# Cross-attention kernel: turned probabilities passed through DRAM, loads in five pieces, stores moved in SP's order

## The chip, the cores and the metric

The kernel runs on one core of a Trainium2 chip. A time is the device time in microseconds of one execution. The kernel before takes 877.26 us, the median of three runs (876.62 to 878.73).

## What is computed

8 batches of 1024 tokens with 640 features attend to 56 text tokens and 8 image tokens, with 20 heads of 32 features and two softmaxes, whose results are added:

```python
q = _split_heads(hidden_states @ w_q, HEADS)
k, v = _split_heads(text @ w_k, HEADS), _split_heads(text @ w_v, HEADS)
out_text = _merge_heads(_sdpa(q, k, v))
k_ip, v_ip = _split_heads(ip_h @ w_k_ip, HEADS), _split_heads(ip_h @ w_v_ip, HEADS)
out_ip = _merge_heads(_sdpa(q, k_ip, v_ip, mask=mask_ip))
out = (out_text + IP_SCALE * out_ip) @ w_out + b_out + residual
```

## The kernel before, in words

**Groups.** The work is cut into NG = 16 groups of GQ = 512 tokens, two for each batch (GPB = 2). Features lie on the partitions. The 640 features are KD = 5 blocks of 128, and each block holds four heads. A matmul of full precision is made of three (L99 to L102): every operand is split into a high part, rounded by ACT, and a low part, the difference, taken by DVE or POOL.

**Chunks.** The scores of one block of features are a chunk of `prob`: 128 tokens on the partitions, 1024 columns (4 token tiles, 4 heads, 64 keys). A chunk m of group g goes through ACT (`copy_scores`, L203), POOL (mask and `sub_max`, L243, L249), DVE (`maxima`, L216), ACT (`exponentials`, L208), DVE (`sums`, L222) and POOL (`normalise`, L256). The product with V needs keys on the partitions, so the chunk must be turned. `turn` (DVE, L229 to L237) transposes it in squares of 32 into a slot of `stage`, and `hand_over` (SP, L454 to L463) moves the squares to their partitions by DMA, back into the chunk's place in `prob`. It does this in three shares, `SHARES`: chunks 0 and 1, chunks 2 and 3, chunk 4. Each share takes 16 DMAs (4 source quadrants by 4 target quadrants), and one semaphore for each share, `pT_landed`, is met when all 16 have landed.

**After landing.** For each of ten pairs of heads (p = 2m, 2m + 1), `pT_part` on ACT (L717 to L720) waits for the share, rounds the pair into `pT_hi` (ring of 4), and POOL (L573, odd p) or DVE (L946, even p) writes `pT_lo`. `pv_pair` on PE (L1166, L1167) multiplies both with `v_parts`. `move_pv` (ACT, L725) and `add_pv` (DVE, L956) put the pair together, `oT_part` on ACT (L729) and POOL (L569) splits it, and `out_step` on PE multiplies with the output weights. `output` on DVE (L958 to L962) adds bias and residual into `res`, and SP stores it.

**One pass of PE's loop** (L1205 to L1227), for group g: pairs 0 and 1 of group g, the scores of chunk 0 of g + 1, the rest of the output product of g - 1 (39 wide matmuls), then four times two pairs, the scores of the next chunk, 9 output matmuls of g and 15 query matmuls of g + 2, and 15 more query matmuls at the end. So the softmax of g + 1 runs beside the products of g, and the pass of g + 1 begins with the pairs of its chunk 0.

**Every engine's order is written by hand.** DVE in a pass: the low parts of x for g + 2, outputs of g - 1, `turn(g, 4)` (L1001), then `turn(n, 0)` and `turn(n, 1)` of n = g + 1 (L1012, L1013), `turn(n, 2)` (L1028), and at the end `pT_part(n, 0)`, `pT_part(n, 2)`, `turn(n, 3)` (L1030 to L1032). SP, which issues nearly all DMAs, in a pass:

```python
hand_over(g, 2)                      # chunk 4 of g
for m in OUT_ORDER: store(g - 1, m)  # five stores, each waits for its output
...                                  # first pass of a batch: load_k, load_v
hand_over(g + 1, 0)                  # chunks 0 and 1
load_x(g + 3); load_res(g)           # one DMA of 1280 KB each
hand_over(g + 1, 1)                  # chunks 2 and 3
```

`load_x(g)` waits for the low parts of the x that had the buffer before (L466); `load_res(g)` waits for all stores before it (L470). A wait on SP holds everything queued behind it.

Of the kernel before, what the change touches and what calls it, by code (L numbers as in the profile page):

```python
# [5 lines left out]
F32 = mybir.dt.float32  # L6
F32R = mybir.dt.float32r
ACT = mybir.ActivationFunctionType
ALU = mybir.AluOpType
# [17 lines left out]
S_RING = 4  # L27


def attention_kernel(nc, xT_dram, textT, ipT, bbox, w_q, w_k, w_v, w_k_ip, w_v_ip, w_out, b_out, grid_x, grid_y, outT):  # L30
# [24 lines left out]
    k_scratch = nc.dram_tensor("k_scratch", (P, B, KD * KEYS), F32).ap()  # L55
    v_scratch = nc.dram_tensor("v_scratch", (TT, D), F32).ap()
# [3 lines left out]
    with whole:  # L60
# [108 lines left out]
        res_loaded, stored = sem("res_loaded"), sem("stored")  # L169

        SHARES = ((0, 2), (2, 4), (4, 5))
        pT_landed = [sem(f"pT_landed{i}") for i in range(len(SHARES))]

        def landed(eng, g, m):

            share = min(m // 2, len(SHARES) - 1)
            wait(eng, pT_landed[share], 16 * QUADS * QUADS * (g + 1))
# [48 lines left out]
        def stage_slot(m):  # L226
            return min(m, S_RING - 1)

        def turn(dve, g, m):  # L229

            before = (g, 3) if m == 4 else (g - 1, 4) if m == 3 else (g - 1, m)
            dve.wait_ge(prob_done, KD * g + m + 1)
            if before[0] >= 0:
                landed(dve, *before)
            src = prob[:, m * CHUNK:(m + 1) * CHUNK].rearrange("p (t c i) -> p t c i", t=GT, i=QUAD)
            dst = stage[:, stage_slot(m)].rearrange("p c (t i) -> p t c i", i=QUAD)
            nc.vector.transpose(dst, src).then_inc(turned, 1)  # L237
# [43 lines left out]
        stage = sb("stage", [P, S_RING, 2 * QUADS, P])  # L281
# [104 lines left out]
        def pT(p):  # L386

            return prob[:, p * GQ:(p + 1) * GQ]

        def pT_at(t, g, p):  # L390
            return t[:, (PAIRS * g + p) % P_RING, :]

# [23 lines left out]
        with nc.Block() as block:  # L416

            @block.sync
            def _(sp):
# [34 lines left out]
                def hand_over(g, share):  # L454
                    m0, m1 = SHARES[share]
                    turns = stage[:].rearrange("p s (h c) t -> p (s h) c t", c=QUADS)
                    pairs = prob[:].rearrange("p (n q t) -> p n q t", q=QUADS, t=P)
                    s0 = 2 * stage_slot(m0)
                    sp.wait_ge(turned, KD * g + m1)
                    for q in range(QUADS):  # L460
                        for c in range(QUADS):
                            sp.dma_start(pairs[c * QUAD:(c + 1) * QUAD, 2 * m0:2 * m1, q, :],  # L462
# [803 lines left out]
```

## Time and profile before

| what | value |
| --- | --- |
| median of the runs | 877.26 us |
| profiled execution | 873.89 us |
| its span, first to last instruction | 872.1 us |
| PE busy (matmul) | 814.0 us, 93% |
| DVE, POOL, ACT busy | 670.6, 624.1, 541.3 us |
| mean granted TensorE clock | 0.976 |
| DMA moved | 128.08 MB, mean 147 GB/s |

The profile is of one execution. Busy time is time in which an engine works on an instruction; issuing a DMA doesn't count as busy, and stands under SPq in the chain and in the timeline. The idle time of an engine is put down to what released it. The chain is the path of work that ended last, followed back step by step. A granted clock of 1.00 is 2.4 GHz, half of it 1.2 GHz.

### The profile page before, as it was taken

To read this page: it belongs to the slowest core of one execution; us is meant where nothing else is said; L and a number is where in the kernel's file an instruction comes from. 1 tells how busy PE (TensorE), PEld (TensorE's weight loads), DVE (VectorE), ACT (ScalarE), POOL (GpSimd) and SP (SyncE) were. 2 spreads that over 40 slices of the span, in tenths; PEclk is the share of its full clock that TensorE was granted. 3 is DMA by queue.
4 is the path that set the end of the run, shared out by engine and by line. 5 is a ranking of instruction groups with operands and counts; after the bars stand their busy time and mean duration, and the time that the engine had idled before them with its cause. 6 is when DMAs were issued, how large, how long until landed. Compare 5 with 4: busy or idle time off the path is not lost.

```text
span 872.1 us, 13091 instructions
## 1 busy us (share of the span) xinstructions
PE 814.0 (93%) x4381; PEld 650.9 (75%) x4381; DVE 670.6 (77%) x983; ACT 541.3 (62%) x928; POOL 624.1 (72%) x576
## 2 busy tenths in 40 slices
PE   9999779999989998999989998999989998998586
PEld 8899558787868776787868776887867786885464
DVE  7758578888868796888868796888868796987853
ACT  7766267675766666665656666667757666675531
POOL 0069349696959786787959786887959697887841
PEclk9999989999999999899999999999999999999898
DMA  9933343536362725446462726445463626252525
GB/s 324 378 94 119 108 126 89 176 115 187 113 194 52 232 57 165 143 120 181 120 192 57 225 55 182 130 127 170 133 192 100 191 88 212 58 177 62 176 61 193
DMA packets 138867, 128.08 MB, mean 147 GB/s; under 512 B 17072, under 2 KB 101040, under 8 KB 138672
## 3 DMA queue, kind: packets, MB, share of 16 engines
q1 hardware_dynamic: 138656, 125.93, 48.4%
q10 hardware_dynamic: 144, 1.31, 0.4%
q8 instruction: 35, 0.57, 0.3%
q14 instruction: 32, 0.26, 0.1%
HBM read 61.32 MB, written 23.59 MB: 97 GB/s over the span
## 4 chain that ended last, share of the span: by engine, by line
SPq 45%; DVE 17%; PE 15%; DMA 11%; issue 7%; ACT 4%; POOL 1%; ACTq 0%; DVEq 0%
SPq L462 39%; DMA xin<-in_xT 6%; DVE res L962 4%; SPq L497 4%; DVE xT_lo L117 3%; PE bank L100 3%; DVE stage L237 3%; PE bank L101 3%; PE bank L102 3%; DMA res<-in_xT 2%; DVE o_raw L956 2%; DMA prob<-stage 2%; PE bank L196 1%; ACT xT_hi L113 1%; DVE top L216 1%
## 5 line engine op out<-in xcount | busy, mean ns | idle before, releaser
L573 POOL TENSOR_TENSOR pT_lo<-prob,pT_hi 128x512 fp32r<-128x512 f32 x80 | 116.4, 1455 | 99.9 <-ACT pT_hi L720 99.6
L725 ACT ACTIVATE pv_part<-bank 64x512 f32<-64x512 f32 x160 | 94.7, 592 | 148.2 <-PE bank L1167 145.8
L249 POOL TENSOR_TENSOR prob<-prob,top 128x896 f32<-128x896 f32 (+1 forms) x160 | 179.4, 1142 | 4.5 <-DVE top L216 4.1
L256 POOL TENSOR_TENSOR prob<-prob,inv 128x896 f32<-128x896 f32 (+1 forms) x160 | 172.6, 1101 | 11.3 <-DVE inv L224 10.6
L100 PE MATMUL bank<-oT_hi,wo_hi 128*128 128x512 f32 x400 | 168.9, 422 | 8.3 <-POOL oT_lo L569 4.7
L100 PE MATMUL bank<-xT_hi,wq_hi 128*128 128x512 f32 x400 | 156.0, 390 | 5.8 <-ACT qT L139 3.2
L101 PE MATMUL bank<-oT_lo,wo_hi 128*128 128x512 f32 x400 | 159.1, 398 | 0.0
L102 PE MATMUL bank<-oT_hi,wo_lo 128*128 128x512 f32 x400 | 158.6, 396 | 0.0
L101 PE MATMUL bank<-xT_lo,wq_hi 128*128 128x512 f32 x400 | 155.6, 389 | 0.0
L102 PE MATMUL bank<-xT_hi,wq_lo 128*128 128x512 f32 x400 | 155.6, 389 | 0.0
L569 POOL TENSOR_TENSOR oT_lo<-o_raw,oT_hi 128x512 fp32r<-128x512 f32 x80 | 109.9, 1374 | 61.9 <-ACT oT_hi L729 60.6
L956 DVE TENSOR_TENSOR o_raw<-bank,pv_part 64x512 f32<-64x512 f32 x160 | 110.1, 688 | 55.6 <-ACT pv_part L725 52.8
L720 ACT ACTIVATE pT_hi<-prob 128x512 fp32r<-128x512 f32 x160 | 93.4, 623 | 78.0 <-DMA prob<-stage 77.2
L946 DVE TENSOR_TENSOR pT_lo<-prob,pT_hi 128x512 fp32r<-128x512 f32 x80 | 73.5, 919 | 56.3 <-ACT pT_hi L720 55.3
L222 DVE TENSOR_REDUCE total<-prob 128x16 f32<-128x896 f32 (+1 forms) x160 | 101.7, 676 | 4.4 <-ACT prob L208 4.2
L100 PEld LDWEIGHTS bank<-oT_hi,wo_hi 128*128 128x128 f32 x400 | 76.8, 192 | 36.6 <-ACT prob L203 7.3
L1166 PE MATMUL bank<-pT_hi,v_parts 128*128 128x512 f32 x160 | 67.5, 422 | 38.9 <-DVE pT_lo L946 28.4
L196 PEld LDWEIGHTS bank<-k_diag,qT 64*128 64x128 f32 x1280 | 81.7, 196 | 28.7 <-issue 21.4
L216 DVE TENSOR_REDUCE top<-prob 128x16 f32<-128x896 f32 (+1 forms) x160 | 99.6, 664 | 2.1 <-POOL prob L243 1.3
L237 DVE STREAM_TRANSPOSE stage<-prob 128x1024 f32<-128x1024 f32 x80 | 97.2, 1224 | 1.4
L196 PE MATMUL bank<-k_diag,qT 64*128 64x128 f32 x1280 | 97.0, 294 | 0.1
L203 ACT ACTIVATE prob<-bank 128x512 f32<-128x512 f32 x160 | 85.5, 592 | 11.3 <-PE bank L196 11.1
(103 smaller groups left out, 1247.8 us busy)
## 6 DMA issues: line engine op xcount, KB each, us to landing
prob<-stage SPq DMA_DIRECT2D x512, 64.0 KB, 2.0
res<-in_xT SPq DMA_DIRECT2D x16, 1280.0 KB, 9.3
outT<-res SPq DMA_DIRECT2D x80, 256.0 KB, 2.6
xin<-in_xT SPq DMA_DIRECT2D x15, 1280.0 KB, 6.3
prob<-stage SPq DMA_DIRECT2D x256, 32.0 KB, 1.9
w_raw<-in_L_xattn_w_k SPq DMA_DIRECT2D x8, 320.0 KB, 4.9
w_raw<-in_L_xattn_w_k_ip SPq DMA_DIRECT2D x8, 320.0 KB, 5.3
w_raw<-in_L_xattn_w_v_ip SPq DMA_DIRECT2D x8, 320.0 KB, 4.3
```

Of the source, the lines that this page charges most:

```text
L100: nc.tensor.matmul(dst, a_hi, b_hi, start=first, stop=False)
L101: nc.tensor.matmul(dst, a_hi, b_lo, start=False, stop=False)
L102: return nc.tensor.matmul(dst, a_lo, b_hi, start=False, stop=last)
L196: ins = nc.tensor.matmul(s_bank(g, 2 * m + r)[:, t * PW:(t + 1) * PW], qT[rows, m, q_cols], k_diag[rows, m, :], start=True, stop=True)
L216: ins = nc.vector.tensor_reduce(top[:, m, n, :], chunk(m)[:, :, k0:k1], AX.X, ALU.max)
L237: nc.vector.transpose(dst, src).then_inc(turned, 1)
L249: ins = nc.gpsimd.tensor_tensor(s, s, top[:, m, n, :].unsqueeze(2).broadcast_to([P, ROWS, k1 - k0]), ALU.subtract)
L256: ins = nc.gpsimd.tensor_tensor(s, s, inv[:, m, n, :].unsqueeze(2).broadcast_to([P, ROWS, k1 - k0]), ALU.mult)
L462: sp.dma_start(pairs[c * QUAD:(c + 1) * QUAD, 2 * m0:2 * m1, q, :], turns[q * QUAD:(q + 1) * QUAD, s0:s0 + 2 * (m1 - m0), c, :]).then_inc( ...
L569: nc.gpsimd.tensor_tensor(oT_at(oT_lo, g, m), o_raw[:, (KD * g + m) % 2, :], oT_at(oT_hi, g, m).bitcast(F32), ALU.subtract).then_inc(oT_lo ...
L573: nc.gpsimd.tensor_tensor(pT_at(pT_lo, g, p), pT(p), pT_at(pT_hi, g, p).bitcast(F32), ALU.subtract).then_inc(pT_lo_pool, 1)
L956: nc.vector.tensor_tensor(by_quadrant(raw), a, c, ALU.add).then_inc(pv_added, 1)
```

## The change

Turned chunks take another way. `write_out` sends one whole stage slot (128 partitions of 4 KB, 512 KB) to a DRAM tensor `p_scratch` in one DMA; `read_back` waits until it has landed and brings it into the chunk's place in four DMAs of 128 KB, one for each quadrant of keys, in runs of 1 KB where `hand_over` before had runs of 512 bytes. To make such runs, `turn` writes its slot in the order quadrant, half, token, and a pair's columns in `prob` are then four runs of 128 instead of one of 512; `pT`, `pT_part_at` and the three `pT_part` follow that. `hand_over` writes all its chunks and then reads them back. There is a `pT_landed` for each chunk. `stage` has three slots in turn instead of four, and `turn` waits for the write of three chunks before (`in_dram`) instead of a landing. The loads of x (from group 2 on) and of the residual are five DMAs each of 256 KB, and stores and residual loads have a semaphore for each block. In SP's pass, `load_x(g + 3)` and the five stores now come ahead of chunk 4's `hand_over`, the residual loads right behind it, and then K and V and the two other `hand_over` calls.

```diff
--- before
+++ after
@@ -24,7 +24,7 @@
 P_RING = 4
-S_RING = 4
+S_RING = 3
@@ -53,6 +53,7 @@
     k_scratch = nc.dram_tensor("k_scratch", (P, B, KD * KEYS), F32).ap()
+    p_scratch = nc.dram_tensor("p_scratch", (KD, P, CHUNK), F32).ap()
     v_scratch = nc.dram_tensor("v_scratch", (TT, D), F32).ap()
@@ -166,15 +167,15 @@
             sem(n) for n in ("mask_added", "max_subbed", "prob_done", "pT_lo_pool", "oT_lo_done"))
-        res_loaded, stored = sem("res_loaded"), sem("stored")
-
-        SHARES = ((0, 2), (2, 4), (4, 5))
-        pT_landed = [sem(f"pT_landed{i}") for i in range(len(SHARES))]
+        res_loaded, stored = [sem(f"res_loaded{m}") for m in range(KD)], [sem(f"stored{m}") for m in range(KD)]
+        written = [sem(f"written{i}") for i in range(S_RING)]
+        pT_landed = [sem(f"pT_landed{m}") for m in range(KD)]
         def landed(eng, g, m):
-
-            share = min(m // 2, len(SHARES) - 1)
-            wait(eng, pT_landed[share], 16 * QUADS * QUADS * (g + 1))
+            wait(eng, pT_landed[m], 16 * QUADS * (g + 1))
+
+        def in_dram(eng, n):
+            wait(eng, written[n % S_RING], 16 * (n // S_RING + 1))
@@ -223,17 +224,13 @@
-        def stage_slot(m):
-            return min(m, S_RING - 1)
-
         def turn(dve, g, m):
-            before = (g, 3) if m == 4 else (g - 1, 4) if m == 3 else (g - 1, m)
-            dve.wait_ge(prob_done, KD * g + m + 1)
-            if before[0] >= 0:
-                landed(dve, *before)
-            src = prob[:, m * CHUNK:(m + 1) * CHUNK].rearrange("p (t c i) -> p t c i", t=GT, i=QUAD)
-            dst = stage[:, stage_slot(m)].rearrange("p c (t i) -> p t c i", i=QUAD)
+            n = KD * g + m
+            dve.wait_ge(prob_done, n + 1)
+            in_dram(dve, n - S_RING)
+            src = prob[:, m * CHUNK:(m + 1) * CHUNK].rearrange("p (t h c i) -> p t h c i", t=GT, h=2, i=QUAD)
+            dst = stage[:, n % S_RING].rearrange("p c h (t i) -> p t h c i", i=QUAD)
             nc.vector.transpose(dst, src).then_inc(turned, 1)
@@ -278,7 +275,7 @@
         v_parts = sb("v_parts", [P, PAIRS, 2, HP], F32R)
-        stage = sb("stage", [P, S_RING, 2 * QUADS, P])
+        stage = sb("stage", [P, S_RING, QUADS, 2, P])
@@ -385,10 +382,14 @@
-            return prob[:, p * GQ:(p + 1) * GQ]
+            m, h = divmod(p, 2)
+            return prob[:, m * CHUNK:(m + 1) * CHUNK].rearrange("p (q h t) -> p q h t", q=QUADS, h=2)[:, :, h, :]
...
             return t[:, (PAIRS * g + p) % P_RING, :]
+
+        def pT_part_at(t, g, p):
+            return pT_at(t, g, p).rearrange("p (q t) -> p q t", q=QUADS)
@@ -451,26 +452,34 @@
-                def hand_over(g, share):
-                    m0, m1 = SHARES[share]
-                    turns = stage[:].rearrange("p s (h c) t -> p (s h) c t", c=QUADS)
-                    pairs = prob[:].rearrange("p (n q t) -> p n q t", q=QUADS, t=P)
-                    s0 = 2 * stage_slot(m0)
-                    sp.wait_ge(turned, KD * g + m1)
-                    for q in range(QUADS):
-                        for c in range(QUADS):
-                            sp.dma_start(pairs[c * QUAD:(c + 1) * QUAD, 2 * m0:2 * m1, q, :],
-                                         turns[q * QUAD:(q + 1) * QUAD, s0:s0 + 2 * (m1 - m0), c, :]).then_inc(pT_landed[share], 16)
+                def write_out(g, m):
+                    n = KD * g + m
+                    sp.wait_ge(turned, n + 1)
+                    wait(sp, pT_landed[m], 16 * QUADS * g)
+                    sp.dma_start(p_scratch[m], stage[:, n % S_RING].rearrange("p c h t -> p (c h t)")).then_inc(written[n % S_RING], 16)
+
+                def read_back(g, m):
+                    in_dram(sp, KD * g + m)
+                    for c in range(QUADS):
+                        sp.dma_start(prob[c * QUAD:(c + 1) * QUAD, m * CHUNK:(m + 1) * CHUNK].rearrange("i (q f) -> i q f", q=QUADS),
+                                     p_scratch[m].rearrange("(q i) (c f) -> c i q f", q=QUADS, c=QUADS)[c]).then_inc(pT_landed[m], 16)
+
+                def hand_over(g, ms):
+                    for m in ms:
+                        write_out(g, m)
+                    for m in ms:
+                        read_back(g, m)
...
                     sp.wait_ge(xT_lo_done, KD * (g - 1))
-                    sp.dma_start(x_of(g), x_half[g % 2, g // 2]).then_inc(x_loaded[g % 2], 16)
-
-                def load_res(g):
-                    wait(sp, stored, 16 * KD * g)
-                    sp.dma_start(res[:], x_half[g % 2, g // 2]).then_inc(res_loaded, 16)
-
-                hand_over(0, 0)
+                    for k in range(KD):
+                        sp.dma_start(x_of(g)[:, k, :], x_half[g % 2, g // 2][:, k, :]).then_inc(x_loaded[g % 2], 16)
+
+                def load_res(g, m):
+                    wait(sp, stored[m], 16 * g)
+                    sp.dma_start(res[:, m, :], x_half[g % 2, g // 2][:, m, :]).then_inc(res_loaded[m], 16)
+
+                hand_over(0, (0, 1))
                 sp.wait_ge(v_ip_added, 2)
@@ -494,10 +503,10 @@
                     sp.wait_ge(out_done, outs_before(g, m) + 1)
-                    sp.dma_start(out_half[g % 2, g // 2, m], res[:, m, :]).then_inc(stored, 16)
+                    sp.dma_start(out_half[g % 2, g // 2, m], res[:, m, :]).then_inc(stored[m], 16)
                 load_x(2)
-                hand_over(0, 1)
+                hand_over(0, (2, 3))
                 sp.wait_ge(v_text_ready, 3 * BLOCKS // 2)
@@ -505,24 +514,25 @@
                     b = g // GPB
-                    hand_over(g, 2)
+                    if g + 3 < NG:
+                        load_x(g + 3)
                     if g > 0:
...
                             store(g - 1, m)
+                    hand_over(g, (4,))
+                    for m in OUT_ORDER:
+                        load_res(g, m)
                     if g % GPB == 0 and b < B - 1:
...
                     if g + 1 < NG:
-                        hand_over(g + 1, 0)
-                    if g + 3 < NG:
-                        load_x(g + 3)
-                    load_res(g)
-                    if g + 1 < NG:
-                        hand_over(g + 1, 1)
+                        hand_over(g + 1, (0, 1))
+                        hand_over(g + 1, (2, 3))
                 for m in OUT_ORDER:
                     store(NG - 1, m)
-                sp.wait_ge(stored, 16 * KD * NG)
+                for m in range(KD):
+                    sp.wait_ge(stored[m], 16 * NG)
@@ -570,7 +580,7 @@
                     pool.wait_ge(pT_hi_done, PAIRS * g + p + 1)
-                    nc.gpsimd.tensor_tensor(pT_at(pT_lo, g, p), pT(p), pT_at(pT_hi, g, p).bitcast(F32), ALU.subtract).then_inc(pT_lo_pool, 1)
+                    nc.gpsimd.tensor_tensor(pT_part_at(pT_lo, g, p), pT(p), pT_part_at(pT_hi, g, p).bitcast(F32), ALU.subtract).then_inc(pT_lo_pool, 1)
@@ -717,7 +727,7 @@
                     wait(act, pv_ready, PAIRS * g + p + 1 - P_RING)
-                    nc.scalar.activation(pT_at(pT_hi, g, p), pT(p), ACT.Copy).then_inc(pT_hi_done, 1)
+                    nc.scalar.activation(pT_part_at(pT_hi, g, p), pT(p), ACT.Copy).then_inc(pT_hi_done, 1)
@@ -730,7 +740,7 @@
                     if k == 0:
-                        act.wait_ge(x_loaded[g % 2], 16 * (g // 2 + 1))
+                        act.wait_ge(x_loaded[g % 2], 16 + 16 * KD * (g // 2))
                         act.wait_ge(q_ready, KD * g)
@@ -943,7 +953,7 @@
                     dve.wait_ge(pT_hi_done, PAIRS * g + p + 1)
-                    nc.vector.tensor_tensor(pT_at(pT_lo, g, p), pT(p), pT_at(pT_hi, g, p).bitcast(F32), ALU.subtract).then_inc(pT_lo_dve, 1)
+                    nc.vector.tensor_tensor(pT_part_at(pT_lo, g, p), pT(p), pT_part_at(pT_hi, g, p).bitcast(F32), ALU.subtract).then_inc(pT_lo_dve, 1)
@@ -956,7 +966,7 @@
                 def output(g, m):
-                    dve.wait_ge(res_loaded, 16 * (g + 1))
+                    dve.wait_ge(res_loaded[m], 16 * (g + 1))
                     dve.wait_ge(out_ready, outs_before(g, m) + 1)
...
                     nc.vector.scalar_tensor_tensor(r, out_bank(g, m)[:], bias[:, m:m + 1], r, ALU.add, ALU.add).then_inc(out_done, 1)
```

## Rows read from the trace of the kernel before

**Rows 1.** Page, part 4: shares of the span, by engine.

```profile
SPq 45%; DVE 17%; PE 15%; DMA 11%; issue 7%; ACT 4%; POOL 1%; ACTq 0%; DVEq 0%
```

**Rows 2.** Stretches: span, busy us (instructions) per engine, PEclk, DMA share, GB/s.

```profile
156.00:203.00 47.00, 46.47 (x255) 36.65 (x253) 40.48 (x58) 31.56 (x55) 38.83 (x37) 1.00 0.50 147
781.00:826.00 45.00, 31.85 (x179) 23.40 (x177) 36.80 (x51) 25.23 (x42) 36.55 (x37) 0.93 0.42 120
826.00:872.10 46.10, 36.33 (x133) 27.52 (x132) 20.30 (x29) 13.27 (x22) 17.00 (x14) 0.87 0.41 131
```

**Rows 3.** Timeline, PE: start us, duration, line, [idle before, releaser].

```profile
156.20 0.39 PE L1166 MATMUL bank<-pT_hi,v_parts 128*128 128x512 f32 x1
...
780.92 0.39 PE L1166 MATMUL bank<-pT_hi,v_parts 128*128 128x512 f32 x1
```

**Rows 4.** Timeline, PE, 425 to 447 us.

```profile
425.00 0.39 PE L1166 MATMUL bank<-pT_hi,v_parts 128*128 128x512 f32 x1
...
432.66 0.39 PE L1166 MATMUL bank<-pT_hi,v_parts 128*128 128x512 f32 x1
...
437.38 0.39 PE L102 MATMUL bank<-xT_hi,wq_lo 128*128 128x512 f32 x1
...
446.53 0.47 PE L1166 MATMUL bank<-pT_hi,v_parts 128*128 128x512 f32 x1 [2.64 <-DVE pT_lo L946]
```

**Rows 5.** Timeline, ACT, 445 us.

```profile
445.03 1.67 ACT L720 ACTIVATE pT_hi<-prob 128x512 fp32r<-128x512 f32 x3 [5.48 <-DMA prob<-stage]
```

**Rows 6.** Waits: who waited for whom, us in total, times, longest.

```profile
ACT pT_hi L720 <- DMA prob<-stage: 77.2, 31, 6.3
...
ACT xT_hi L113 <- DMA xin<-in_xT: 27.3, 14, 4.5
```

**Rows 7.** Timeline, SP's queue, 427 to 444 us.

```profile
427.22 2.65 SPq L497 DMA_DIRECT2D outT<-res  x5
...
432.39 11.18 SPq L462 DMA_DIRECT2D prob<-stage  x16
```

**Rows 8.** Timeline, DVE, 414 to 446 us.

```profile
414.96 1.25 DVE L237 STREAM_TRANSPOSE stage<-prob 128x1024 f32<-128x1024 f32 x1
...
425.51 2.37 DVE L237 STREAM_TRANSPOSE stage<-prob 128x1024 f32<-128x1024 f32 x2
...
445.69 0.69 DVE L946 TENSOR_TENSOR pT_lo<-prob,pT_hi 128x512 fp32r<-128x512 f32 x1 [5.50 <-ACT pT_hi L720]
```

**Rows 9.** Line L462, its issues (ns) and their landing.

```profile
L462 SPq DMA_DIRECT2D prob<-stage x768: 585/601/1712, 90.3 to 853.6; - x192
...
DMA to landing us min/median/max: 1.8/2.0/5.1
```

**Rows 10.** DMA issues: count, size of each, median us to landing.

```profile
res<-in_xT SPq DMA_DIRECT2D x16, 1280.0 KB, 9.3
outT<-res SPq DMA_DIRECT2D x80, 256.0 KB, 2.6
...
k_raw<-k_scratch SPq DMA_DIRECT2D x7, 160.0 KB, 3.7
v_scratch<-v_text SPq DMA_DIRECT2D x1, 960.0 KB, 4.8
```

**Rows 11.** Timeline, SP's queue, 90 us.

```profile
90.35 11.36 SPq L462 DMA_DIRECT2D prob<-stage  x16
```

**Rows 12.** Timeline, ACT, 106 us.

```profile
106.59 0.96 ACT L742 ACTIVATE v_parts<-v_raw 64x320 fp32r<-64x320 f32 x2 [11.11 <-DMA v_raw<-v_ip]
```

**Rows 13.** Timeline, PE, 824 to 857 us.

```profile
824.83 0.76 PE L1166 MATMUL bank<-pT_hi,v_parts 128*128 128x512 f32 x1 [6.51 <-DVE pT_lo L946]
...
856.98 0.47 PE L1166 MATMUL bank<-pT_hi,v_parts 128*128 128x512 f32 x1 [3.54 <-DVE pT_lo L946]
```

**Rows 14.** Timeline, DVE, 842 us.

```profile
842.39 1.25 DVE L237 STREAM_TRANSPOSE stage<-prob 128x1024 f32<-128x1024 f32 x1
```

**Rows 15.** Timeline, ACT, 855 us.

```profile
855.48 1.15 ACT L720 ACTIVATE pT_hi<-prob 128x512 fp32r<-128x512 f32 x2 [4.65 <-DMA prob<-stage]
```

## Prediction

> **What bounds the kernel now.** The page's part 4 comes first: the chain that ended last spends 45% of the span in SP's queue and 15% on PE [rows 1]. The page's engine totals put PE first, so two readings compete, and a table by stretches decides. Over 156 to 203 us PE is busy 46.47 of 47.00 us; over 781 to 826, where no query projection is left, 31.85 of 45.00 [rows 2]. In between a whole group comes round in (780.92 - 156.20) / 13 = 48.05 us [rows 3]. PE's own work in a group is less. One block of it (4 matmuls for a pair of head pairs, 16 small ones for scores, 9 output and 15 query matmuls) takes 432.66 - 425.00 = 7.66 us. From 437.38 PE steps through 27 more wide matmuls and ends 0.39 us after the last, at 443.89 (446.53 less its 2.64 idle): 0.227 us each [rows 4]. A group is three such blocks and two with 15 wide matmuls more: 3 x 7.66 + 2 x 11.06 = 45.1 us. So 3 us of each group are lost, nearly all at its start, where PE waits for DVE's pT_lo.
>
> That wait is followed back. DVE waits for pT_hi, and ACT's pT_hi waited 5.48 us for the landing of prob<-stage at 445.0; ACT was free at 439.55 [rows 5]. All such waits add up to 77.2 us [rows 6]. This landing is the last of 16 DMAs that SP began to issue at 432.39; they stood behind five loads of K and V (this pass begins a batch), 5 stores (2.65 us) and the 16 of the fifth chunk [rows 7]. Yet DVE had ended the turn of the fifth chunk at 416.21, and those of the next group's chunks 0 and 1 at 427.88 [rows 8]. The data were ready 4.5 us before SP reached them. SP is bound by the number of its issues: 768 at L462, 601 ns each and 0.04 between them, against a landing of 2.0 us [rows 9].
>
> **Part by part.** (a) *Fewer issues.* A group's 48 issues become 5 writes and 20 reads. At 0.64 us that is 30.7 against 16.0. Five pieces for x and five for the residual instead of one each add 8 x 0.5 = 4 us. Net, SP issues about 10.7 us less in a group of 48. I price a read at 0.64, as now: as many runs, each twice as long.
>
> (b) *A round trip is added.* SP waits for the write to land before it issues its reads, and behind it in SP's queue stand these reads, the residual loads and the next chunks' writes. No row shows a 512 KB write of this shape. A 256 KB store lands in 2.6 us, 960 KB in 4.8; by size between them 2.6 + 256/704 x 2.2 = 3.4 us; ends 2.0, a landing inside SBUF, and 4.8. The read of 128 KB from DRAM lies between the 2.0 us of the old hand-over and the 3.7 us of k_raw<-k_scratch, 160 KB; I take 3.0 [rows 9, 10].
>
> (c) *The path of a group.* From the end of the fifth turn (416.2): write 0.6 + 3.4, four reads 2.6 (6.6), five residual loads 2.5, SP free at 9.1. The stores are gone from here: they now stand ahead of this turn, and their last output precedes it on DVE, so they cost it nothing. At 11.7 both next turns are done. Chunk 0 was written 1.2 us before; its reads can be issued from 14.5 to 17.1 and land at 20.1. Chunk 1's reads end at 19.7 and land at 22.7. Now the pair lands at 445.0, 28.8 after the turn. ACT asks for chunk 0 at 439.55, 23.3 after the turn, PE for its product at 27.6. Thus chunk 0 has 3 us in hand before ACT and PE has no reason to wait. In the groups that load K and V, five more issues (2.5 us) fit before 11.7.
>
> (d) *What is late next.* Chunks 2 and 3 wait for chunk 3's turn, which stands on DVE (L1032) behind pT_lo, and that sat idle 5.50 us for the same landing [rows 8]. With the idle time gone the turn comes some 3 us sooner against PE's clock; by (b) its last piece lands 9.6 us after the turn, now 12.3. No new wait. The x load: ACT's waits for it add up to 27.3 us [rows 6], at every group's start beside PE's. It is issued behind the 16, at 443.6; after the change it goes out at the head of the pass, ahead of the fifth chunk, some 30 us earlier, and its guard (L466) was met a pass before. The residual load keeps a guard on stores that went out earlier, and is wanted in the next pass.
>
> (e) *Edits without a price.* The split into high and low parts reads four runs of 128 instead of one of 512, and turn writes with one more level of stride. No row shows either; I take 0, with at most 0.2 us for a turn, five of them, under the 5.50 us that DVE idles now. With that cover gone they would cost up to 1 us in a group. A ring of three slots asks for a write three chunks back, which at 9 us or more apart landed long ago.
>
> The sum. *Loop:* 48.05 to 45.5 (45.1 and 0.4 for short waits and a lower clock behind them), 13 x 2.55 = 33.2 us; ends 45.1 and 46.0, the second by the stretch from 156 to 203, where PE idles 0.53 us of 47 and still takes about a microsecond more than 45.1 for its group; so 38 and 27. *Start:* SP's first hand-over takes 11.36 us, and ACT waits 11.11 us for the v_raw that SP issues behind it [rows 11, 12]. Turns end at 89.2 and 90.3; written at 93.2, reads of chunk 0 to 95.8, of chunk 1 to 98.4, against 101.7: 3.3 us; ends 1.9 and 4.0. *Group 14* (780.92 to 824.83, 43.9): DVE is busy 36.80 and POOL 36.55 in this stretch [rows 2]. PE's wait of 6.51 us at its end [rows 13] shrinks only as far as these two allow: 45 less 36.8 leaves 8 us, much of it for PE's own outputs; I give back a third, 2.9; ends 1 and 5. *Group 15:* the fifth turn ends at 843.64; its data reach ACT at 855.48, 11.8 later; after the change 9.6, and the turn itself comes 1.0 sooner, since chunk 2's earlier landing lets the pT_lo ahead of it on DVE go first: 3.2 of the 3.54 us that PE waits at 856.98 [rows 13 to 15]. The granted clock is 0.87 over this last stretch and 1.00 over 156 to 203 [rows 2]; 13% of 36.33 busy us is 4.7 us, and with a shorter wait I count 2.0 of it back: 5.2; ends 2 and 8. Together 33.2 + 3.3 + 2.9 + 5.2 = 44.6 us. The profiled execution took 873.89 us (span 872.1), which becomes 829.3; the median of the runs stands 3.4 above it, so **832.7 us**. With all favourable ends 55 us (822), with all the others 32 (846).
>
> **The rivals.** *Another engine paces the loop.* DVE's 40.48 and POOL's 38.83 busy us of 47 [rows 2] would fall into 45.5, and both serve their queues in order, so a late product on one can reach PE somewhere else. Against: from 425.00 to 443.89 PE runs on without a gap while both keep up [rows 4]. Half a stall stays: 47 us a group, 13 x 1.05 = 13.7, and 9 from start and end: 22.7 saved, 854.6 us.
>
> *The round trip takes more than the issues gave.* Here the end is slower. The place is SP's two waits in a row, for the fifth chunk's write and the next chunk 0's. With a write landing of L, (c) reads 0.6 + L + 2.6 + 2.5, then 0.6 + L + 2.6 + 3.0 = 11.9 + 2L, and it passes today's 28.8 from L = 8.5 us on. Writes stand in the same queue as 1.25 MB of residual load, whose landing is 9.3 us [rows 10]. With L = 9.3 a group is 1.7 us longer, 22 us in all, and the four exposed hand-overs at start and end cost 3.2 each: 912 us. Against: that 9.3 has an x load just ahead of it, which the change takes away, and the write comes 3 us after the residuals.
> By a rule of the Trainium skill (DMA: Bandwidth & Descriptors, "Issuing engines are not separate DMA queues"), the sequencer's time to initiate a DMA is "usually small relative to the DMA itself"; by it the issues saved are worth little, the added trip counts whole, and this rival would hold. The trace disagrees: 10.3 us of issues against 2.0 of landing.
>
> *The change doesn't free PE:* pT_hi could be late for another reason than SP (ACT's order), and the time stays within 0.3% of 877.3. ACT's idle 5.48 us before it speaks against that.
>
> **How the numbers follow.** Forecast 0.63; another engine paces 0.21; round trip 0.07; nothing freed 0.03; better than all favourable ends 0.06. The range leaves out the two cases at and above today's time, most of the 0.06 and, at the slow end, all beyond 856: 821 to 856. About 0.3% (2.6 us) is what a measurement can tell. Faster 0.90, same 0.03, slower 0.07.
>
> **What would show it.** Right: SP's share of the chain falls far below 45% and PE's becomes the largest; groups come round in 45.2 to 45.7; ACT's wait for prob's landing falls from 77.2 to under 20 us and for x from 27.3 to near 0; writes land in 2.6 to 4.8; v_raw lands 3 us earlier. Wrong: writes landing over 6 us, reads over 1 us of issue each, idle PE before L1166 as long as now, or a turn above 1.4 us.

## The result and the profile after

The changed kernel takes 819.84 us, the median of four runs (819.41 to 820.14), against 877.08 us for four runs of the kernel before: 0.934 of its time, 95% interval 0.933 to 0.936. The prediction said 832.7, with a range of 821 to 856. The change saves 57.2 us where 44.6 were forecast, and the time lies 1.2 us under the range.

The page of the kernel after, part 4, shares of the chain by engine:

```profile
PE 88%; POOL 3%; DVE 3%; ACT 2%; SPq 1%; DMA 1%; issue 1%; DVEq 0%; ACTq 0%
```

SP's queue has gone from 45% to 1%, and the chain is PE's own work [rows 1]. Stretches of the same kernel (span, busy us and instructions for each engine, granted clock, DMA share, GB/s): one whole group, then the two last.

```profile
422.50:467.60 45.10, 45.10 (x251) 36.34 (x250) 38.23 (x57) 30.75 (x52) 37.47 (x36) 1.00 0.62 205
738.00:780.00 42.00, 31.35 (x179) 23.57 (x178) 37.80 (x51) 24.80 (x41) 37.51 (x36) 0.96 0.58 188
780.00:818.30 38.30, 32.69 (x134) 25.69 (x133) 21.03 (x29) 13.15 (x22) 17.07 (x14) 0.95 0.52 172
```

PE is busy for all 45.10 us of a group at a clock of 1.00. Where group after group begins, PE's timeline (start, duration, what, idle before):

```profile
151.67 0.39 PE L1176 MATMUL bank<-pT_hi,v_parts 128*128 128x512 f32 x1
...
738.40 0.39 PE L1176 MATMUL bank<-pT_hi,v_parts 128*128 128x512 f32 x1
...
779.75 0.47 PE L1176 MATMUL bank<-pT_hi,v_parts 128*128 128x512 f32 x1 [3.95 <-DVE pT_lo L956]
```

(738.40 - 151.67) / 13 = 45.13 us a group, where it was 48.05 [rows 3]. Each of the thirteen groups takes 45.13 or 45.14. Of the waits, two rows are left that answer to those of before [rows 5, 6]:

```profile
PE bank L1176 <- DVE pT_lo L956: 9.5, 3, 4.0
...
ACT pT_hi L730 <- DMA prob<-p_scratch: 0.9, 1, 0.9
```

ACT's 77.2 us of waiting for the hand-over became 0.9, and its 27.3 us for x has no row any more above 0.2 us. SP's queue over one pass, one that loads K and V:

```profile
564.99 2.33 SPq L476 DMA_DIRECT2D xin<-in_xT  x5
567.36 4.10 SPq L506 DMA_DIRECT2D outT<-res  x5
575.33 0.33 SPq L459 DMA_DIRECT2D p_scratch<-stage  x1
578.21 1.92 SPq L464 DMA_DIRECT2D prob<-p_scratch  x4
580.19 2.33 SPq L480 DMA_DIRECT2D res<-in_xT  x5
582.56 0.43 SPq L153 DMA_DIRECT2D k_raw<-k_scratch  x1
...
585.85 1.47 SPq L459 DMA_DIRECT2D p_scratch<-stage  x2
591.22 4.66 SPq L464 DMA_DIRECT2D prob<-p_scratch  x8
598.34 5.10 SPq L459 DMA_DIRECT2D p_scratch<-stage  x2
603.49 4.34 SPq L464 DMA_DIRECT2D prob<-p_scratch  x8
```

This is the path of the prediction's (c), to be read from chunk 4's write at 575.33: its reads begin at 578.21, the residual loads at 580.19, K and V follow until 584.5, the pair is written from 585.85 and read from 591.22 to 595.88, and lands, by the median of 3.1 us for a read, at 599.0. That is 23.7 us after the turn of chunk 4, and PE begins the next group at 603.00. SP waits 2.9 us for chunk 4's write (575.33 to 578.21), but 5.4 us for the first write of the pair (585.85 to 591.22), which stands behind the residual, K and V. What single issues and landings took (issue in ns; a write of 512 KB, then a read of 128 KB):

```profile
L459 SPq DMA_DIRECT2D p_scratch<-stage x80: 326/338/430, 89.5 to 796.1; - x80
...
DMA to landing us min/median/max: 2.6/3.0/7.0
```

```profile
L464 SPq DMA_DIRECT2D prob<-p_scratch x320: 302/432/1817, 92.1 to 800.1; - x160
...
DMA to landing us min/median/max: 2.3/3.1/4.7
```

A write's landing was estimated at 3.4 and is 3.0 in the median, with 5.4 in the place just shown and 7.0 at most (the prediction had named landings over 6 us as a sign that it was wrong); a read's at 3.0 and is 3.1. A read's issue, priced at 0.64 us like the old hand-over's [rows 9], takes 0.43 and 0.04 between, a write's 0.34.

### The profile page after: what moved, and what is told of

The parts are those of the page before. It is cut to its first block, busy times and chain, and to the rows that moved or that the text cites. A ratio compares the mean times of both kernels' runs of the same rounds, so it can differ in the third digit from the quotient of the medians.

```text
span 818.3 us, 12921 instructions
## 1 busy us (share of the span) xinstructions
PE 795.8 (97%) x4381; PEld 648.8 (79%) x4381; DVE 676.2 (83%) x983; ACT 541.3 (66%) x928; POOL 627.7 (77%) x576
## 4 chain that ended last, share of the span: by engine, by line
PE 88%; POOL 3%; DVE 3%; ACT 2%; SPq 1%; DMA 1%; issue 1%; DVEq 0%; ACTq 0%
PE bank L101 23%; PE bank L102 21%; PE bank L103 21%; PE bank L197 10%; PE bank L1176 4%; PE bank L1177 4%; PE bank L1061 1%; PE bank L1069 1%; PE bank L1073 1%; POOL prob L246 1%; POOL oT_lo L579 1%; DMA xin<-in_xT 1%; POOL pT_lo L583 1%; DVE wo_lo L846 1%; POOL prob L253 1%
## 5 line engine op out<-in xcount | busy, mean ns | idle before, releaser
L246 POOL TENSOR_TENSOR prob<-prob,top 128x896 f32<-128x896 f32 (+1 forms) x160 | 184.0, 1170 | 14.8 <-DVE top L217 14.7
L253 POOL TENSOR_TENSOR prob<-prob,inv 128x896 f32<-128x896 f32 (+1 forms) x160 | 170.3, 1086 | 11.6 <-DVE inv L225 10.4
L101 PE MATMUL bank<-oT_hi,wo_hi 128*128 128x512 f32 x400 | 165.9, 415 | 3.6 <-POOL oT_lo L579 3.6
L197 PEld LDWEIGHTS bank<-k_diag,qT 64*128 64x128 f32 x1280 | 79.1, 190 | 27.6 <-issue 21.5
L197 PE MATMUL bank<-k_diag,qT 64*128 64x128 f32 x1280 | 94.0, 288 | 0.2 <-ACT prob L204 0.2
L209 ACT ACTIVATE prob<-prob 128x1024 f32<-128x1024 f32 x80 | 84.4, 1055 | 10.8 <-POOL prob L246 10.1
L101 PEld LDWEIGHTS bank<-xT_hi,wq_hi 128*128 128x128 f32 x400 | 75.6, 189 | 18.7 <-DVE v_ip L938 2.9
```

What stands on the lines that cost most here:

```text
L101: nc.tensor.matmul(dst, a_hi, b_hi, start=first, stop=False)
L197: ins = nc.tensor.matmul(s_bank(g, 2 * m + r)[:, t * PW:(t + 1) * PW], qT[rows, m, q_cols], k_diag[rows, m, :], start=True, stop=True)
L246: ins = nc.gpsimd.tensor_tensor(s, s, top[:, m, n, :].unsqueeze(2).broadcast_to([P, ROWS, k1 - k0]), ALU.subtract)
L253: ins = nc.gpsimd.tensor_tensor(s, s, inv[:, m, n, :].unsqueeze(2).broadcast_to([P, ROWS, k1 - k0]), ALU.mult)
```

## Experiments

Group times below are read from PE's timeline as above. All kernels are told against the kernel before on the same chip.

### The two halves: order alone, route alone

`order_only` is the kernel before with this edit of SP's pass:

```diff
-                    hand_over(g, 2)
+                    if g + 3 < NG:
+                        load_x(g + 3)
                     if g > 0:
                         for m in OUT_ORDER:
                             store(g - 1, m)
+                    hand_over(g, 2)
+                    load_res(g)
...
-                    if g + 3 < NG:
-                        load_x(g + 3)
-                    load_res(g)
```

> The kernel before with SP's new order alone: x load and stores ahead of chunk 4's hand-over, the residual load right behind it; hand-over still 16 DMAs a share inside SBUF, loads in one piece. Theory A (the number of issues bounds SP, 48 of 0.64 us in a group): the issues are unchanged, so groups still lose about half of their 3 us; a group comes round in 46.5 us or more, time 855 to 865. Theory B (what counts is only what stands between chunk 4's turn and the next pair's landing): stores (2.65 us) leave this path and the x load no longer stands behind the pair, so the path is 28.8 - 2.65 = 26.1 us against the 27.6 at which PE asks; the loop comes to 45.1 to 45.5 us, time 832 to 840, with start and end as before (first hand-over 11.4 us, ACT's last wait for the landing over 3 us).

It takes 842.79 us, ratio 0.961 (0.956 to 0.965), groups of 45.90 us on average, between 45.13 and 47.43. Its chain:

```profile
PE 42%; SPq 30%; DVE 10%; issue 5%; DMA 5%; POOL 4%; ACT 4%; ACTq 0%; DVEq 0%
```

Neither theory had it right. Theory A's 46.5 us or more is wrong. Theory B had the size of the loop nearly (45.9 for 45.1 to 45.5), but SP kept 30% of the chain. With 48 issues, order alone gives 2.15 of the 2.92 us in a group, and nothing at the start and 1.9 us in the last two groups.

`route_only` is the changed kernel with SP's old order and whole loads:

```diff
-                    if g + 3 < NG:
-                        load_x(g + 3)
+                    hand_over(g, (4,))
                     if g > 0:
                         for m in OUT_ORDER:
                             store(g - 1, m)
-                    hand_over(g, (4,))
-                    for m in OUT_ORDER:
-                        load_res(g, m)
...
                         hand_over(g + 1, (0, 1))
+                    if g + 3 < NG:
+                        load_x(g + 3)
+                    load_res(g)
+                    if g + 1 < NG:
                         hand_over(g + 1, (2, 3))
```

> The changed kernel with SP's old order and x and residual loads in one piece: only the way through DRAM (5 writes, 20 reads in a group) is kept. Theory A: the issues fall, all of the loop's gain is here; 45.1 to 45.3 us a group, 820 to 823. Theory B: chunk 4's hand-over is 5 us of SP, stores 2.65 and K and V 2.5 fit before the next pair is turned at 11.7, and the x load is issued some 18 us after the turn and lands before PE's 27.6; also 45.1 to 45.5 and 820 to 826. A rival: the x load still arrives late at each group's start; then ACT's waits for x stay at 15 us or more and the time is 830 or more.

It takes 819.10 us, ratio 0.933 (0.929 to 0.938): the whole gain, with groups of 45.13. No wait for x above 0.2 us is left. So the way through DRAM does it alone, and the new order adds nothing that can be measured on top of it; each of the two relieves the same path, and their gains don't add.

`x_first` moves only the x load of the kernel before to the head of the pass.

```diff
+                    if g + 3 < NG:
+                        load_x(g + 3)
                     hand_over(g, 2)
...
-                    if g + 3 < NG:
-                        load_x(g + 3)
```

> The kernel before with one move: the x load goes to the head of SP's pass. Stores still stand between chunk 4 and the next pair, issues are unchanged. If the odd passes of before, which hardly wait for the pair (0.2 to 0.5 us), were long because x landed late, they come down and the others stay: loop of 47.0 us, 860 to 866. If stores and chunk 4 in front of the pair are all of it, the time stays at 873 or more; if x alone made it, it is near order_only's 842.8 with 45.9 us a group.

870.30 us, ratio 0.990 (0.982 to 0.997), 47.58 us a group. The kernel's waits (us in total, times, longest):

```profile
ACT pT_hi L720 <- DMA prob<-stage: 80.8, 29, 6.3
...
ACT xT_hi L113 <- DMA xin<-in_xT: 4.5, 1, 4.5
```

The wait for x fell from 27.3 to 4.5 us [rows 6], the one for the hand-over stayed, and a group got only 0.5 us shorter. Over thirteen groups that is 6 us, less than the 11 over which the runs of the kernel before spread, so how much x alone is worth stays open. It was read right that x was late, and it was a small part: the pair's landing came last in most groups. The passes that hardly wait for the pair did not come down as expected. Here is one of them (span, PE busy first, then the other engines, clock, DMA share, GB/s):

```profile
445.14:492.62 47.48, 47.03 (x250) 37.62 (x251) 39.79 (x58) 31.22 (x55) 40.10 (x36) 0.96 0.49 144
```

It is long because PE is busy longer, at a clock below 1.00, and not because x is late; the section on the prediction comes back to this. One thing `x_first` settles: the row "PE bank L100 <- ACT prob L203", 3.5 us in nine waits in the kernel before, is gone here. These short waits of PE came from ACT's lateness with x.

### Loads in five pieces

`whole_loads` is the changed kernel with `x_of(g)` and `res` loaded in one DMA each:

```diff
-                    for k in range(KD):
-                        sp.dma_start(x_of(g)[:, k, :], x_half[g % 2, g // 2][:, k, :]).then_inc(x_loaded[g % 2], 16)
+                    sp.dma_start(x_of(g), x_half[g % 2, g // 2]).then_inc(x_loaded[g % 2], 16)
```

> The changed kernel with x and residual loads as one DMA of 1280 KB each instead of five of 256 KB. Both are wanted as a whole (x) or a pass later (residual), and SP has time: same time within 0.3% (817.5 to 822.5), groups at 45.13 us. If pieces matter, it is at the start, where x for group 2 is waited for: up to 2 us longer or shorter there.

819.02 us, ratio 0.933 (0.929 to 0.938), groups of 45.13. As expected, the pieces change nothing.

### Issues put back: eight and sixteen reads

`reads8` reads each chunk back in eight DMAs of 64 KB, `reads16` in sixteen of 32 KB:

```diff
                     for c in range(QUADS):
-                        sp.dma_start(prob[...].rearrange("i (q f) -> i q f", q=QUADS),
-                                     p_scratch[m].rearrange("(q i) (c f) -> c i q f", q=QUADS, c=QUADS)[c]) ...
+                        for h in range(2):
+                            sp.dma_start(prob[...].rearrange("i (q h f) -> i q h f", q=QUADS, h=2)[:, :, h],
+                                         p_scratch[m].rearrange("(q i) (c h f) -> c h i q f", q=QUADS, c=QUADS, h=2)[c, h]) ...
```

> The changed kernel with each chunk read back in eight DMAs of 64 KB (runs of 512 bytes) instead of four: 45 issues for the hand-over of a group, nearly the 48 of before, but still through DRAM and in the new order. A read's issue took 432 ns after the change; 20 more in a group are about 9.5 us, 4 or 5 of them in the pair's path. If the number of issues is what counts, the group grows past 45.5 us. If slack covers it (the pair now lands about 4 us before PE asks), the loop stays at 45.1 to 45.3 and only the exposed hand-overs at start and end cost 1 to 2 us each: 820 to 825.

859.75 us (two runs), ratio 0.978 (0.967 to 0.988), groups from 45.13 to 51.25 us, 47.59 on average. I had expected that slack would cover it. Three pieces of the chain of `reads8` (start, us, what), and PE's scores after them:

```profile
506.97 4.74 DMA p_scratch<-stage
...
519.81 6.22 DMA p_scratch<-stage
...
533.86 2.04 DMA prob<-p_scratch
```

```profile
538.09 1.16 PE L197 MATMUL bank<-k_diag,qT 64*128 64x128 f32 x16 [2.66 <-ACT qT L140]
```

The turn of chunk 4 ended at 506.96. Its write landed in 4.74 us and not in 3.0, for it stands in the queue behind x and the stores; the pair's write took 6.22 us behind the residual, K and V, where it took 5.4 in the changed kernel. The sixteen reads end at 533.86, the last lands 2.04 later, 28.9 us after the turn, and PE waited 2.66 us. So the prediction's path is the right one, and the slack on it is about 4 us (23.7 against 27.6). What I missed is that a late SP can lengthen its own landings: once writes are ready before SP comes to them, they go out right behind its loads. In the pass shown the two waits for writes are 2.7 us longer together than in the changed kernel (11.0 against 8.3). They are not all of the loss: of the 32 us by which the thirteen groups are longer than 586.7, PE idled 21.4 and was busy 10.6 us longer, with a clock of 0.93 to 0.97 in four of them.

Beside `order_only` this run says what the way through DRAM costs by itself. With the same order and nearly the same number of issues for the hand-over (45 and 48), the direct way takes 45.90 us a group and the detour 47.59, on two chips. So the detour as such gives nothing; it gains because it can be made with fewer issues.

> The same with sixteen reads of 32 KB for each chunk: 85 issues for the hand-over and 100 in all in a group, at 0.43 to 0.47 us 43 to 47 us of SP in a group of 45.1. Theory (SP's issues bounded the kernel before and are what the change took away): SP's queue is the chain again, a group takes 47 us or more, 845 to 890. If the DMA engines or the landings bounded it instead, the time stays under 830.

1127.07 us, ratio 1.28. Its chain:

```profile
SPq 60%; DMA 21%; PE 8%; issue 7%; DVE 3%; ACT 1%; POOL 0%; DVEq 0%; ACTq 0%
```

As the issue theory has it, only stronger, for the waits for writes come on top of the issues: 18% of the chain, and SP can do nothing else in them. By an estimate from this run's rows, 100 issues of 0.46 us and three waits of 5.9 us, the median landing of a write here, are 64 us; a group took 64.34. The reads keep their runs of 1 KB and their bytes, so only their number has changed. PE itself was busy 75 us longer in the thirteen groups than the 586.7 of the changed kernel, while its clock stood at 0.84 to 0.90.

### Longer trips

`longer2` sends the slot twice more to a spare tensor before every chunk's reads and waits each time; `trip_4` does it once and for chunk 4 only, `trip_4_0` once for chunks 4 and 0:

```diff
                 def read_back(g, m):
                     in_dram(sp, KD * g + m)
+                    for _ in range(m in (4, 0)):
+                        trips[0] += 1
+                        sp.dma_start(d_scratch, stage[:, (KD * g + m) % S_RING].rearrange("p c h t -> p (c h t)")).then_inc(again, 16)
+                        sp.wait_ge(again, 16 * trips[0])
```

> The changed kernel with each wait for a written chunk made longer: before the reads of a chunk SP sends the stage slot twice more to a spare DRAM tensor and waits for each landing, so L, the wait for a write, is some 10 us instead of 3.0. It also moves 5 MB more in a group. The prediction's rival put the turning point at L = 8.5 us, for the path of chunk 4 and the next chunk 0; two further waits stand in SP's queue. Expected with my path: chunk 0 lands 9 us later than now, about 5 us after PE asks, so groups of 49 to 52 us, 880 to 920. If the pair has more slack than I reckon, under 47 us a group.

1156.67 us, ratio 1.32, far beyond what I expected:

```profile
DMA 62%; SPq 23%; PE 7%; issue 4%; DVE 3%; ACT 1%; POOL 0%; DVEq 0%; ACTq 0%
```

The chain is landings. I had counted two waits in a pass and there are five, with two trips of 2.6 us and more in each: ten trips are over 26 us in a pass.

> The changed kernel with one more write to a spare DRAM tensor, waited for, ahead of chunk 4's reads only (3.0 + 0.3 us more of SP). Path theory (from chunk 4's turn: write, trip, reads, residual loads 2.3, K and V 2.0, then the pair): the added 3.3 us end at 10.7 or 12.7 us after the turn, when the next pair is turned at 11.7; the pair lands at most 1 us later than its 23.7, PE asks at 27.6: loop 45.13 to 45.3, time 819 to 822. If SP's whole cycle is what is full, the time is 830 or more.

822.48 us (820.98 and 823.99), ratio 0.938 (0.932 to 0.944). In the profiled execution, the shorter of the two, eleven of thirteen groups are at 45.13 or 45.14, the two others at 45.6 and 45.8, 45.22 on average. The path theory holds for the loop: 3 us more before the pair is turned cost it 1.1 us in thirteen groups. The last group, with nothing to hide them behind, takes 40.3 us instead of 38.6.

> The same with a second trip ahead of chunk 0's reads, so that both waits of the prediction's rival are about doubled. Path theory: in passes that load K and V the pair lands 28 to 29 us after chunk 4's turn instead of 23.7, one to two us later than PE can take; these groups (half) grow by 1 to 3 us, the others by under 1: loop 45.6 to 46.8, time 826 to 842. If a write's landing were all that counted, with 8.5 us as the turning point the prediction gave (6.3 here), nothing would change: under 822.

848.30 us (844.43 and 852.16), ratio 0.967 (0.961 to 0.974), 47.11 us a group in the longer of the two. Its waits:

```profile
ACT pT_hi L736 <- DMA prob<-p_scratch: 59.4, 31, 4.5
...
PE bank L199 <- ACT qT L141: 10.3, 11, 1.7
```

The direction is as the path theory says, and its turning point lies between one trip more and two. The size is not: 2 us a group where I expected 0.5 to 1.7. The pattern is not either: the groups grow up to the ninth and shrink again (45.1, 45.9, 47.1, 46.4, 46.9, 48.7, 49.4, 47.8, 50.1, 46.3, 47.1, 45.5, 46.2), and those whose pass loads K and V, every second one from 45.9 on, are not the longer ones. The median landing of a write rose to 4.1 us, as in `reads8`. In the thirteen groups PE idled 17.0 us and was busy 8.8 us longer, most of it in the groups of 49.4 and 50.1 us, at a clock of 0.93. How much longer landings and the clock each add to the path isn't separated by these runs.

### Start and end

`early_start` issues the x load of group 2 ahead of the first hand-over, and the V loads between the first writes and their reads:

```diff
+                load_x(2)
-                hand_over(0, (0, 1))
+                for m in (0, 1):
+                    write_out(0, m)
                 sp.wait_ge(v_ip_added, 2)
...
+                for m in (0, 1):
+                    read_back(0, m)
```

> The changed kernel with two moves at the start: the x load of group 2 is issued ahead of the first hand-over instead of behind the V stores, and the V loads between the first two writes and their reads. If ACT's wait for x (4.4 us on DVE at 111.6) and for v_raw (3.8 us) set the start, PE's waits before group 1 go and group 1 begins 2 to 5 us sooner: 815 to 818. If PE's own work or its lower clock sets it, within 1 us of 819.8.

817.54 us, ratio 0.932 (0.927 to 0.937). Group 1 begins at 147.82 instead of 151.67 in the profiled executions. Part of that is the execution: this one is the shortest of four, and in `early_tail`, with the same start, group 1 begins at 149.72, against 151.26 for the changed kernel on that chip. On its own chip `early_start` overlaps with `whole_loads` (819.02, from 816.94 to 820.53), so its gain, some 2 us, is in the expected range but not clear of the spread.

`early_tail` adds this on DVE:

```diff
                         sums(dve, n, 3)
+                        if n == NG - 1:
+                            pT_part(n, 0)
                         turn(dve, n, 2)
                         maxima(dve, n, 4)
-                        pT_part(n, 0)
+                        if n < NG - 1:
+                            pT_part(n, 0)
```

> early_start with one more move: for the last group DVE makes pT_lo of pair 0 ahead of the turn of chunk 2 and of maxima of chunk 4. PE waits 3.95 us for this pT_lo at the last group's start. If DVE's order is what holds it, the last group begins 1 to 2.4 us sooner and the time is 1 to 2 us below early_start's 817.5: 815 to 816.5. If the landing of the pair or the later turn decides, no change from 817.5.

PE's first pair of the last group, in `early_start` and then in `early_tail`:

```profile
775.91 0.67 PE L1179 MATMUL bank<-pT_hi,v_parts 128*128 128x512 f32 x1 [3.98 <-DVE pT_lo L959]
```

```profile
776.23 0.47 PE L1182 MATMUL bank<-pT_hi,v_parts 128*128 128x512 f32 x1 [1.23 <-DVE pT_lo L959]
```

The wait fell from 3.98 to 1.23 us, and group 14 from 41.36 to 39.78. In six runs it takes 816.51 us (816.05 to 819.13), against 819.73 (818.47 to 819.84) for the changed kernel on the same chip: the fastest kernel here. Both moves together are worth 3.2 us. Against `early_start` alone the times (another chip) can't tell 1 us; the group's length can.

> The changed kernel itself, to have it on the same chip as the others and in more runs. Its loop is PE's own work to 0.01 us (45.13 us in every group), so its runs should lie within 2 us of each other (818 to 821), while the kernel before, whose length hangs on SP's queue, spreads over 6 us or more. If that spread is the chip's and not the kernel's, both spread alike.

819.73 us in six runs, 818.47 to 819.84, and eleven runs of the kernel before beside them from 871.07 to 881.97. The same chip gives one kernel a spread of 1.4 us and the other 10.9. So the spread isn't the chip's. What makes it isn't settled: it looks natural to lay it on SP's queue, but `order_only` (2.3 us in four runs) and `x_first` (1.5 in two) hang on that queue too and spread little. The clock goes with it: the three longest of the eleven (879.31 to 881.97) show a mean granted clock of 0.967, the two shortest 0.971 and 0.972.

## Why the prediction missed, step by step

The mechanism held for the most part: SP's queue was the bound, issues fell, the round trip fits, PE's own work is what is left. The rivals didn't come true. What failed are terms of the sum. The largest is the 0.4 us a group that the loop was left with, "for short waits and a lower clock behind them": 4.8 us, measured 0. After it come group 15 (3.5 us too small), the base (3.4) and the start (1.2).

**Base.** I took 44.6 us off a median that stood 3.4 us above the profiled execution. The spans of the two profiled executions differ by 872.1 - 818.3 = 53.8 us, and the medians by 57.2: the profiled execution of before was one of its faster ones (its runs lie between 871 and 883 us in all), and that of after is not. 3.4 us of the miss are this.

**Loop**, forecast 33.2, measured 624.7 - 586.7 = 38.0 us. PE's own work, 45.1, was right. The 0.4 for short waits and a lower clock was not. The thirteen groups, before and after (span, then busy us and instructions of PE, its weight loads, DVE, ACT and POOL, granted clock, DMA share, GB/s):

```profile
156.20:780.92 624.72, 602.59 (x3251) 475.66 (x3250) 502.49 (x730) 404.76 (x690) 493.52 (x456) 0.99 0.49 142
```

```profile
151.67:738.40 586.73, 586.73 (x3251) 472.84 (x3250) 506.76 (x729) 404.59 (x688) 495.29 (x456) 1.00 0.65 207
```

After the change PE does not idle in them at all, and its clock is 1.00. This term alone is 4.8 us. My own favourable end, 38, was the value.

The rows before also show that the loss was misread. I laid the 3 us of a group nearly all on PE's wait at its start. PE's waits in these groups were:

```profile
PE bank L1166 <- DVE pT_lo L946: 14.0, 7, 3.4
PE bank L1166 <- POOL pT_lo L573: 4.2, 10, 0.5
PE bank L100 <- ACT prob L203: 3.5, 9, 0.6
```

Of the 38.0 us only 22.1 were idle time, 18.2 of them before pairs. The other 15.9 were PE being busy longer with the same 3251 matmuls. More than half of that comes with a low clock. The group that begins at 348.04 behind a wait of 3.42 us idles 0.46 us and still takes 49.01 (all of it, then a stretch near its start):

```profile
348.04:397.05 49.01, 48.55 (x251) 38.36 (x251) 39.82 (x57) 30.75 (x53) 38.49 (x36) 0.93 0.47 136
350.00:354.00 4.00, 4.00 (x21) 3.17 (x21) 2.64 (x4) 2.60 (x5) 4.00 (x4) 0.50 1.05 393
```

Four such groups (clock 0.93 to 0.96, each behind a wait of 2.16 to 3.42 us) were busy 9.3 us longer than 45.13 each. What makes the other 6.5 us, at a clock of 1.00, isn't shown. So the effect that I kept hung on causes that the change removes: the low clock came behind the waits for the pair, and the short waits on scores, by `x_first`, from the late x, which (d) said would go.

**Start**, forecast 3.3: group 0 begins 1.9 us earlier (110.00), less than expected, but group 0 itself takes 41.67 us instead of 44.29. I gave group 0 nothing. x for group 2 is in use at 110.90 instead of 117.07. Together 4.5. The stretch behind it still ran at a low clock:

```profile
112.00:125.00 13.00, 10.81 (x47) 8.11 (x44) 11.25 (x16) 10.35 (x19) 8.06 (x8) 0.74 0.74 225
```

With `early_start` group 1 begins 3.9 us sooner still.

**Group 14**, forecast 2.9, measured 43.91 - 41.35 = 2.6: DVE is busy 37.80 of 42 us, as the term said.

**Group 15**, forecast 5.2, measured 47.3 - 38.6 = 8.7 (span's end less 779.75). DVE's last turn and ACT's use of its data:

```profile
794.87 1.25 DVE L234 STREAM_TRANSPOSE stage<-prob 128x1024 f32<-128x1024 f32 x1
```

```profile
803.35 1.15 ACT L730 ACTIVATE pT_hi<-prob 128x512 fp32r<-128x512 f32 x2
```

The turn ends 16.4 us into the group (18.8 before), not 1.0 but 2.4 sooner, and the data are in use 7.2 us later (11.8 before), not 9.6: in an empty queue the write landed in 2.6 us and four reads took 1.75 to issue, not 2.6. PE's wait of 3.54 us [rows 13] is gone altogether, and with it the low clock: from the start of this pair's first matmul to the end of the span it is 12.5 us (805.77 to 818.3) and was 15.1. The granted clock over the last stretch is 0.95 instead of 0.87 [rows 2].

The sum of what was measured is 38.0 + 4.5 + 2.6 + 8.7 = 53.8, and 3.4 of base makes 57.2. Against the forecast that is 4.8 + 1.2 - 0.3 + 3.5 + 3.4 = 12.6 of the 12.9 us missed.

**Edits without a price (e).** Nothing was the right price: in the median a turn takes 1232 ns before and after, and a `pT_hi` 620 and 623.

**Round trip as a rival.** It turned out to have a point where it decides, as written, but not as a constant. The prediction put it at 8.5 us of landing, with 3.4 taken for what a write costs wherever it stands. The runs show landings from 2.6 to 7.0 us by what is queued ahead; the two waits of the path add up to 8.3 us in the pass shown above, not to 6.8. Cheaper issues (0.47 us a read instead of 0.64) made up for it, and the pair landed 23.7 us after the turn where 22.7 was forecast. One trip of 3 us more was hidden in the loop, two were not. The rule of the Trainium skill that was weighed there (DMA: Bandwidth & Descriptors, "Issuing engines are not separate DMA queues") is not borne out here: with the same bytes, 80 instead of 20 reads in a group cost 307 us (1127.07 against 819.84), with the longer landings and the lower clock that followed.

## What to carry to other kernels

When one queue issues many small transfers, price its issues before its bytes: here a detour through DRAM with 25 issues in a group beats a direct way with 48. Ask for each wait in such a queue what is queued ahead of the transfer, for its landing is no constant, and a queue that falls behind makes its own landings longer. Where the bound moves to an engine that runs without a gap, take its own work as the forecast, and drop every short wait, and every low clock behind a wait, whose cause the change removes. Before calling a loss a wait, compare the busy time of the same instructions too: here two fifths of it stood there.

## What the runs showed of the hardware

- The issue of a DMA on SP's queue did not go by its bytes. In the median it took 338 ns for 512 KB in 128 whole rows, 432, 432 and 421 ns for reads from DRAM of 128, 64 and 32 KB, 430 ns for 256 KB of residual, 601 ns for the old hand-over's 64 and 32 KB inside SBUF. Shape isn't all of it either: the same 1280 KB load of x took 594 ns in the kernel before and 432 in `whole_loads` and `route_only`. What it hangs on besides isn't shown.
- The landing of a 512 KB write took 2.6 us in an empty queue and up to 7.0 behind loads.
- Writing 2.6 MB to DRAM and reading them back in each group, at a DMA share of 0.65 instead of 0.49 over the thirteen groups, cost PE nothing.
- TensorE's granted clock was 0.50 over 350 to 354 us of the kernel before, behind a wait of 3.42 us, and 1.00 in all thirteen groups of the changed kernel, in which PE never waits.
- Kernels whose loop is PE's own work repeated within 0.7 to 3.6 us on a chip; the kernel before spread over 11 on one.
